# Layer 0: the wrap round of the older row's base bank, ahead of the cosine rounds in the upper tiles

## What is computed

```
def _gn(v, G=8, eps=1e-5): ...            # mean and variance over a group of 2 channels
# layer 0
X = jnp.fft.rfftn(gn(x), axes=(-2, -1));  Xr, Xi = real(X), imag(X)
Yr = _rconv(Xr, wr) - _rconv(Xi, wi) + b_real[:, None, None]     # 3x3, pad 1, on the spectrum
Yi = _rconv(Xr, wi) + _rconv(Xi, wr) + b_imag[:, None, None]
x = x + jnp.fft.irfftn(lax.complex(Yr, Yi), axes=(-2, -1))
# layer 1
x = x + mean_filter_15x15(_gn(x))
```

## Time and profile before

| | us |
|---|---|
| median of 3 runs | 3748.55 |
| lowest and highest of the 3 | 3742.32, 3749.32 |
| the profiled execution's own time | 3746.19 |
| its span, first to last instruction | 3744.4 |
| busy in the span: PE, DVE, POOL, ACT | 3342.5, 3183.2, 2595.3, 2111.4 |
| mean granted share of TensorE's clock | 0.963 |

### The profile page before, as it was taken

The page is one execution under the profiler, slowest core; times in us unless marked ns, Lnnn a source line. Parts: engine busy times, 40 slices in busy tenths (PEclk is TensorE's granted clock), DMA queues, the critical chain, the costliest instruction groups (busy, mean ns, idle before and its releaser), DMA issues.

```text
span 3744.4 us, 114575 instructions
## 1 busy us (share of the span) xinstructions
PE 3342.5 (89%) x38496; PEld 2211.3 (59%) x38496; DVE 3183.2 (85%) x5926; ACT 2111.4 (56%) x4286; POOL 2595.3 (69%) x2121
## 2 busy tenths in 40 slices
PE   3189989998999989999898998999899998999988
PEld 1045566555765557655675556755476555765567
DVE  6889978898779988899788997889977998879976
ACT  0068832786338852488426883278733786238842
POOL 5069953898539966499645995389943996639964
PEclk9589999999999999999999999999999999999999
DMA  7456657664776638666485664856467663866634
GB/s 185 158 114 127 123 153 221 108 128 94 206 185 124 128 84 245 152 127 129 121 235 121 127 128 141 234 103 129 98 192 195 119 128 82 238 159 126 129 86 136
DMA packets 720057, 544.18 MB, mean 145 GB/s; under 512 B 589696, under 2 KB 665056, under 8 KB 707424
## 3 DMA queue, kind: packets, MB, share of 16 engines
q1 hardware_dynamic: 697312, 422.30, 48.9%
q10 hardware_dynamic: 22400, 117.46, 11.8%
HBM read 258.41 MB, written 148.90 MB: 109 GB/s over the span
## 4 chain that ended last, share of the span: by engine, by line
PE 78%; DVE 11%; issue 4%; ACT 2%; DMA 2%; POOL 1%; SPq 1%; ACTq 1%; DVEq 0%; POOLq 0%
PE p L567 25%; PE h_ps L679 14%; PE h_ps L477 9%; PE h_odd L477 9%; PE p L705 6%; PE p L516 4%; PE p L574 3%; PE h_ps L567 2%; DVE stat L995 2%; DVE ob_all L1252 2%; PE p L485 1%; ACT arena L748 1%; DVE ob_all L1006 1%; PE h_ps L574 1%; ACTq L888 1%
## 5 line engine op out<-in xcount | busy, mean ns | idle before, releaser
L567 PE MATMUL p<-arena,bd_all 64*64 64x512 f16 x16896 | 1291.3, 381 | 33.4 <-DVE ob_all L1174 23.1
L1376 POOL TENSOR_TENSOR arena<-img 128x512 f32<-128x512 f32 x392 | 499.1, 1274 | 459.4 <-PE h_ps L679 437.3
L567 PEld LDWEIGHTS p<-arena,bd_all 64*64 64x64 f16 x16896 | 552.2, 105 | 380.2 <-issue 239.3
L748 ACT ACTIVATE arena<-h_ps 128x512 f16<-128x512 f32 x512 | 305.8, 597 | 834.4 <-PE h_ps L679 599.3
L1327 POOL TENSOR_TENSOR ob_all<-ob_all,img 128x512 f32<-128x512 f32 x512 | 664.2, 1297 | 86.3 <-DVE ob_all L1168 59.6
L1330 POOL TENSOR_TENSOR ob_all<-ob_all 128x512 f32<-128x512 f32 x512 | 654.1, 1278 | 40.1
L679 PE MATMUL h_ps<-bd_all,arena 128*128 128x128 f32 x3584 | 539.5, 286 | 0.0
L1236 DVE TENSOR_TENSOR arena<-h_ps,arena 128x512 f16<-128x512 f32 x512 | 353.2, 690 | 207.0 <-ACT arena L748 205.5
L679 PEld LDWEIGHTS h_ps<-bd_all,arena 128*128 128x128 f32 x3584 | 447.6, 191 | 121.2 <-issue 115.4
L1168 DVE SCALAR_TENSOR_TENSOR ob_all<-p,bias_c,cosw 128x256 f32<-128x256 f32 x1024 | 447.5, 478 | 57.1 <-PE p L567 19.8
L805 ACT ACTIVATE img<-img,half_row (+1 forms) x1024 | 486.5, 527 | 4.8
(11 more groups left out here) (168 smaller groups left out, 5008.6 us busy)
## 6 DMA issues: line engine op xcount, KB each, us to landing
out<-ob_all SPq DMA_DIRECT2D x512, 256.0 KB, 4.2
bd_all<-bd_dram SPq DMA_DIRECT2D x512, 224.0 KB, 2.6
img<-in_x ACTq DMA_DIRECT2D x168, 512.0 KB, 7.1
img<-in_x ACTq DMA_DIRECT2D x112, 256.0 KB, 4.8
img<-in_x SPq DMA_DIRECT2D x24, 512.0 KB, 23.6
bd_dram<-ob_all SPq DMA_DIRECT2D x16, 768.0 KB, 3.5
arena<-arena SPq DMA_TRANSPOSE x512, 2.7
xT_more<-arena SPq DMA_TRANSPOSE x512, 2.7
```

The costliest lines, as they stand in the source:

```text
L567: m = mm(bank[out_half * HP:(out_half + 1) * HP, :], bd[s % RB][rows, 6 * lm + (j if own else j + 1), :], part, start=opens and i3 == 0, s ...
L1376: G.tensor_tensor(diff[u % 2], img[:, u + R, :], img[:, u - R - 1, :], ALU.subtract).then_inc(moved, 1)
```

## The change

```diff
 LOWER = [("base", 0), ("base", 1), ("cosine", 0), ("cosine", 1), ("cosine", 2),
          ("base", 2), ("wrap", 3), ("sine", 0), ("sine", 1), ("sine", 2)]
 UPPER = [("base", 0), ("base", 1), ("sine", 0), ("sine", 1), ("sine", 2),
-         ("base", 2), ("cosine", 0), ("cosine", 1), ("cosine", 2), ("wrap", 3)]
+         ("base", 2), ("wrap", 3), ("cosine", 0), ("cosine", 1), ("cosine", 2)]
```

## The result

| | before | changed |
|---|---|---|
| median of 6 runs, us | 3747.97 | 3813.28 |
| lowest and highest | 3742.32, 3752.41 | 3810.35, 3818.65 |
| ratio to before, with its 95% interval | | 1.0173 [1.0162, 1.0185] |

A forecast was written before the change was run, and what follows sets the result against it. Two equal 3.84 us cycles, PE's own and one through DVE, bound layer 0's loop rows; 3.7 - 0.3 + 0.25 = 3.65 an image, 29 for eight, on 3746.2 gives 3775, kept as 3776, range 3764 to 3796.

The forecast's parts named there:

- Two cycles without slack in the loop: Layer 0 loop rows: PE's own cycle and the one through DVE (L1168, round 2, p1_ready) both take 3.84 us.
- 0.15 of slack in the written-out rows: Layer 0 rows outside the loop: DVE's part takes 1.90 us, against its fixed price of 1.75, so that cycle has slack.
- The bounds of what is left of the stall are 0 and 0.12; I take 0: PE's 0.12 us wait for p1_half at round 6 vanishes, as the wait moves to round 7; PE's cycle falls to 3.72.
- The signal that comes second: p1_ready, set right behind p2_ready in round 9, comes about 26 ns later; loop rows would cost 0.12 each, time near 3784.
- The move of p1_ready: From round 8 to round 9: plus 0.216, minus the 0.12 stall, 0.096 us later; loop rows 3.94.
- Rows by kind: Per image: 38 loop rows +3.7 us, rows with L1205 0, 14 written-out rows -0.3, between the kinds +0.25.
- The stall in round 7: Slower rival, chance 0.07: both half-bank waits hold PE as one did, loop rows 4.06, 3822 us; half gives some 3799.
- some 0.03 left: Bound in the range: 0.03 us of the stall remaining in a row, adding 9 us to the time.
- faster rival: Chance 0.08: p1_ready does not release L1168, so its delay costs nothing; POOL is next at some 3.78 a row, 3723 us.
- the rows that named POOL or L1126: Evidence for the faster rival: L1126 ends 0.10 us before L1168; a written-out row has it 0.26 after POOL's L1330.

The follow-up runs named there:

- The late signal: Kernel before, its order of rounds kept, with p1_ready set by the first matmul of round 9 instead of the last of round 8: 3809.7 us, 1.0156.
- the last run: Kernel before with LOWER's cosine rounds first, t1_done's and t2_done's waits parted, and UPPER's cosine rounds one round sooner: 3701.03 us, 0.9872.

## Why the prediction was wrong

Point by point, by its own steps.

**What bounds the kernel: right.** Two cycles without slack in the loop, 0.15 of slack in the written-out rows, none of it mattering where L1205 makes DVE late. The late signal shows the cycle through DVE, the last run PE's own.

**"The bounds of what is left of the stall are 0 and 0.12; I take 0": the first step that failed.** It left 0.065 a row. The prediction put the loader's release at 1203.41 by one wait instruction of 0.051 "with as much again between", 0.03 before it was needed. Two things are wrong in that. The second wait costs 0.14 to 0.15 and not 0.10. And 1203.41 is the time of a load, while 1203.44 is when round 7's first matmul should start; that comes 0.03 behind its load (1203.31 and 1203.34), so the 0.03 of room was none. With 0.15 the load is at 1203.46 and the matmul at 1203.49, 0.05 late, close to the 0.065 measured. None of the rows read shows the distance of the waits, but the trace of before has it: the loader's first load behind the second wait, in the row whose first load behind the first wait is at 1203.31, is

```profile
1203.46 0.10 PEld L567 LDWEIGHTS p<-arena,bd_all 64*64 64x64 f16 x1
```

One wait in place of two gave back 0.061 a row and 27 us.

**The signal that comes second: in the text, left out of the sum.** The Trainium skill's "TensorE: Matmul & The Clock Gate", section "The cost: per-tile semaphore tail", has such signals about 26 ns apart, and the prediction gave 3784 by it. The trace agrees: 0.287 in place of 0.257 from the end of the matmul to L1168, and 0.03 a row, 10 us, back when the order in round 9 was turned. It holds here for two pairs of 64x64 matmuls.

**The move of p1_ready, 0.096 a row: right**, within 0.015. With both other terms taken out the kernel took 3778.7. So the mechanism was right, and its size was off by the two terms: 3776 + 27 + 10 is the 3813 that was measured.

**Rows by kind: right.** L1205's rows did not move. The written-out rows lost 0.08 where a gain of 0.025 was forecast; the two missing terms of 0.065 and 0.025 are that difference, nearly.

**The rivals.** The stall in round 7 was named, with 3822 for all of it and 3799 for half. Half of it came, plus the signal. Its price in the range was set at "some 0.03 left" and 9 us, without a reason for 0.03 and for the loop's rows alone. The range already held 8 for the signal and 3 for the written-out rows; with 27 for the stall it would have reached 3814. Its lower end doesn't follow from its bounds either: 3776 - 9 is 3767 and not 3764. No faster rival held: the rows that named POOL or L1126 as what precedes L1168 showed neighbours in time, not causes.

## What to carry to other kernels

Where two cycles run at the same length, taking a stall out of one gains nothing if the same edit lengthens the other: ask of each moved instruction what signal it carries and who starts on it. Count the wait instructions at one place: here two, one behind the other, held PE for 0.065 where one held it for nothing. Of two signals set in one place, set the one that is waited for first; it was worth 0.03 a row here. Look for the wait that names too much: PE waited for both of DVE's reads ahead of rounds of which one half needed only the first. With the two waits parted and the lower half's cosine rounds first, the stall was gone and the kernel 28 us faster than before, and with p1_ready a round sooner 49 us.

## What the runs showed that was not expected

A second wait instruction on PE, behind one that has just been met, costs 0.14 to 0.15 us, though its record lasts 0.051. And POOL's three instructions, 3.76 us in sum, fit into rows of 3.70, since L1329 starts before the record of L1322 has ended. Its timeline in the fastest kernel (there L1322, L1329 and L1332 are the L1320, L1327 and L1330 of before):

```profile
1203.41 1.17 POOL L1322 TENSOR_TENSOR arena<-g_more,arena 128x512 f16<-128x512 f32 x1
1204.53 1.31 POOL L1329 TENSOR_TENSOR ob_all<-ob_all,img 128x512 f32<-128x512 f32 x1
1205.92 1.28 POOL L1332 TENSOR_TENSOR ob_all<-ob_all 128x512 f32<-128x512 f32 x1
1207.15 1.17 POOL L1322 TENSOR_TENSOR arena<-arena 128x512 f16<-128x512 f32 x1
```

From 1203.41 to 1207.15 is 3.74 for this row, and the 30 rows have 3.70 on average: a sum of durations is not a floor.
